# Two attention stages of a gated cross-attention block: rows on ScalarE's queue, ten pooled blocks, the maxima behind the value products

## The chip, the cores and the metric

The kernel runs on one core of one Trainium2 chip. The metric is the device time of one execution in microseconds; the time before is the median of three runs. The trace is of one further execution under the hardware profiler. TensorE does matmuls, VectorE, ScalarE and GpSimd the rest, and the sequencers of SyncE (SP) and GpSimd issue the DMAs.

## The reference

Two layers, each an attention and a mixture of experts, on x of 2 x 1024 x 512 in float32. Only the attention matters here. There are 16 heads of 32. Layer 0 adds a causal self-attention (1024 keys) and a cross-attention on a context of 2048 tokens; layer 1 has a cross-attention alone:

```python
att = einsum('bhqd,bhkd->bhqk', q, k) * scale
y   = einsum('bhqk,bhkd->bhqd', softmax(where(causal, att, -inf)), v)
y   = y + einsum('bhqk,bhkd->bhqd', softmax(einsum(qc, kc) * scale), vc)
```

## The kernel before, in words

The program runs in stages: projections, attention of layer 0 (`attn0`), its output and routing, experts, and the same for layer 1 (`attn1`). The change is in `attention` and in the class `Job`; both attention stages run it.

A unit is four heads of one batch entry. `attn0` has 16 units, causal and cross in turn; `attn1` has 8 cross units. A unit has four jobs of 256 queries, a job has steps of two key blocks of 128: a cross job has 8 steps, the causal jobs 1, 2, 3 and 4. That is 336 steps in `attn0` and 256 in `attn1`. The class `Plan` fixes, by an order written ahead of time, at which step each further piece of work is done.

In a step TensorE computes four score groups s0 to s3 (`scores`, L704): for one key block and two heads each, keys by queries, transposed, into one of three PSUM banks (`SC` = 3). The masks of the causal diagonal are added by small matmuls (L707). ScalarE takes the exponential of each bank into `probs` (L780), a ring of three steps (`RING`). A score group waits until the exponential three items back has left its bank; s2 of a step thus waits for the exponential of s3 of the step before. The step's value products (`values`, L721) follow one step late: four heads side by side in the array for each block, and after them, with a matrix of ones as weights (L728), the sums of the probabilities. Blocks listed in `job.pooled` have no ones products: GpSimd adds their probabilities up (L655, L658), and one ones group at the job's end (L736) takes the total in, after a wait for the last add. In the count of instructions each of these float32 matmuls is two, so that a group of four heads is eight.

The exponential needs the largest score of each query. TensorE computes scores a second time in another layout (`maxima`, L674, in PSUM `mx`, one buffer), and VectorE reduces them (L810). One group of maxima is 128 queries by up to 512 keys of four heads. The plan gives most steps one group, some two, the last none. They stand between s1 and s2. Two steps after a job's last group its maxima are turned by TensorE (`turn`, L687), written to SBUF by ScalarE (`turned`, L768), and set by DMA as an additional row, row 96, of the queries (`set_row`, L587), which stands against a row of ones in the keys. The first score group of a job waits for that row (L697). A drain of the job's sums (`drain`, L789), reciprocals (L827) and a product on GpSimd (L635) end a job.

SP issues, in its own order, the loads of the next units (`load_flat` for the maxima, `load_stack` in ten pieces for scores and values), the stores of results, and the rows. It holds no work of its own, but each issue stands behind the one before it and behind their waits.

Of the kernel before, what the change touches and what calls it, by code (L numbers as in the profile page):

```python
# [19 lines left out]
F32 = mybir.dt.float32  # L20
# [8 lines left out]
P = 128  # L29
B, T, D = 2, 1024, 512  # L30
TC, CC = 2048, 256
HEADS, HD = 16, 32
GH = P // HD
NG = HEADS // GH
UNITS = B * NG
BLK = 512
# [7 lines left out]
DMA = 16  # L44


class Phase:


    def __init__(self, nc, name):  # L50
        self.nc, self.name, self.stack, self.sems = nc, name, ExitStack(), []
# [329 lines left out]
QB = 256  # L381
STEP = 2
LEAD = 4
BUFS, TOPS, ROWS_DEEP = 2, 4, 10
# [9 lines left out]
class Job:  # L394
# [3 lines left out]
    def __init__(self, unit, u, qb, first):  # L398
        self.unit, self.u, self.qb, self.first = unit, u, qb, first
        if unit.causal:  # L400
            d = 2 * qb
            self.blocks = [(kb, 0, False) for kb in range(d)] + [(d, 0, True), (d + 1, P, True)]
        else:
            self.blocks = [(kb, 0, False) for kb in range(unit.keys // P)]
        self.steps = len(self.blocks) // STEP
        self.last = first + self.steps - 1
        self.groups = []
        for t in range(QB // P):
            n = (qb * (QB // P) + t + 1) * P if unit.causal else unit.keys
            self.parts = -(-n // BLK)  # L410
            for part in range(self.parts):
                cols = min(BLK, n - part * BLK)
                self.groups.append((t, part, cols, unit.causal and part == self.parts - 1))
        whole = [kb for kb, n0, masked in self.blocks if not masked]
        inner = [kb for kb in whole if kb < len(self.blocks) - 3]
        self.pooled = [kb for kb in inner if kb < 2 or kb % 2 == 0] if len(inner) > 2 else []

    def adds(self, step=None):

# [93 lines left out]
def attention(nc, name, c, units):  # L513
# [4 lines left out]
    plan = Plan(units)  # L518
    jobs, N_STEPS, N_JOBS = plan.jobs, plan.steps, len(plan.jobs)
# [3 lines left out]
    with Phase(nc, name) as ph:  # L523
        KS = [ph.sb(f"keys{b}", [P, GH, KEYS], F32R) for b in range(BUFS)]
        QS = [ph.sb(f"queries{b}", [P, GH, T], F32R) for b in range(BUFS)]
# [7 lines left out]
        topT = ph.sb("topT", [ROWS, TOPS, P], F32R)  # L533
# [12 lines left out]
        row_set = [ph.sem(f"row_set{d}") for d in range(ROWS_DEEP)]  # L546
        inverted = [ph.sem(f"inverted{d}") for d in range(DEEP)]
        y_out = [ph.sem(f"y_out{d}") for d in range(DEEP)]
        FLAT, STACK, ROW, PIECES = 2, 10, QB // P, 4

        def load_flat(sp, u, piece):
            unit, b = units[u], u % BUFS
            if piece == 0:
                sp.dma_start(KN[b][:, 0:unit.keys].bitcast(F32), unit.k_src[unit.row, :, 0, :]).then_inc(flat_in[b], DMA)
            else:
                sp.dma_start(QN[b][:, :].bitcast(F32), unit.q_src[unit.row, :, 0, :]).then_inc(flat_in[b], DMA)
# [20 lines left out]
        with nc.Block() as block:  # L577
            @block.sync
            def _(sp):
                def set_row(j):  # L580
                    job = jobs[j]
                    sp.wait_ge(exped, plan.turn_item[j] + 1)
                    if job.u >= BUFS:
                        sp.wait_ge(valued, plan.last_of[job.u - BUFS] + 1)
                    q0 = job.qb * QB
                    for t in range(QB // P):
                        sp.dma_start(QS[job.u % BUFS][3 * HD:3 * HD + 1, :, q0 + t * P:q0 + (t + 1) * P].bitcast(F32),  # L587
                                     topT[t * GH:(t + 1) * GH, j % TOPS, :].bitcast(F32)
                                     ).then_inc(row_set[j % ROWS_DEEP], DMA)

                def store(j):
                    d, job = j % DEEP, jobs[j]
                    sp.wait_ge(normed, j + 1)
                    sp.dma_start(job.unit.y_dst[job.unit.row, :, job.qb * QB:(job.qb + 1) * QB], y[d][:, :]
                                 ).then_inc(y_out[d], DMA)

                for piece in range(FLAT):
                    load_flat(sp, 0, piece)
                for piece in range(STACK):
                    load_stack(sp, 0, piece)  # L600
                for piece in range(FLAT):
                    load_flat(sp, 1, piece)
                for j in plan.turn_at[-1]:
                    set_row(j)
                for piece in range(STACK):
                    load_stack(sp, 1, piece)
                for m in range(N_STEPS + 8):
                    if 0 <= m - 7 < N_STEPS and plan.ends(m - 7) is not None:
                        store(plan.ends(m - 7))
                    for j in plan.turn_at.get(m, ()):  # L610
                        set_row(j)
                    for u in range(len(units) - BUFS):
                        piece = m - max(plan.unit_max_at[u], 0) - 1
                        if 0 <= piece < FLAT:
                            sp.wait_ge(max_ready, plan.unit_groups[u])
                            load_flat(sp, u + BUFS, piece)
                        for piece in range(2 * (m - plan.last_of[u] - 1), 2 * (m - plan.last_of[u])):
                            if 0 <= piece < STACK:
                                sp.wait_ge(valued, plan.last_of[u] + 1)
                                load_stack(sp, u + BUFS, piece)  # L620
                for d in range(DEEP):
                    sp.wait_ge(y_out[d], DMA * len(range(d, N_JOBS, DEEP)))
# [39 lines left out]
            def _(pe):  # L662
# [83 lines left out]
                    turn(j)  # L746
                for m in range(N_STEPS + 1):
                    if m < N_STEPS:
                        scores(m, 0)
                        scores(m, 1)  # L750
                        for k in plan.groups_at[m]:
                            maxima(k)
                        scores(m, 2)
                    if m:
                        values(m - 1)
                    if m < N_STEPS:
                        for j in plan.turn_at[m]:
                            turn(j)
                        scores(m, 3)

            @block.scalar
            def _(act):
                def turned(j):
                    item = plan.turn_item[j]
                    act.wait_ge(scored, item + 1)
                    if j >= TOPS:
                        act.wait_ge(row_set[(j - TOPS) % ROWS_DEEP], ROW * DMA * ((j - TOPS) // ROWS_DEEP + 1))
                    act.activation(topT[:, j % TOPS, :], sc[0:ROWS, item % SC, 0:P], ACT.Copy, scale=-1.0  # L768
                                   ).then_inc(exped, 1)

                def exponent(m, i):
                    job, item = jobs[plan.job_of[m]], plan.item[m, i]
                    _, n0, _ = job.blocks[(m - job.first) * STEP + i // 2]
                    if m >= RING and i == 0:
                        act.wait_ge(valued, m - RING + 1)
                        if plan.adds(m - RING + 1):
                            act.wait_ge(added, plan.adds(m - RING + 1))
                    act.wait_ge(scored, item + 1)
                    heads = slice(2 * (i % 2), 2 * (i % 2) + 2)
                    act.activation(probs[:, m % RING, i // 2, heads, n0:],  # L780
                                   sc[:, item % SC, :].rearrange("p (h q) -> p h q", q=QB)[:, :, n0:],
                                   ACT.Exp, scale=SCALE).then_inc(exped, 1)

                def drain(j):
                    d = j % DEEP
                    act.wait_ge(job_done, j + 1)
                    if j >= DEEP:
                        act.wait_ge(normed, j - DEEP + 1)
                    act.activation(both[d][:, :, :], acc[:, :, :], ACT.Copy).then_inc(drained, 1)  # L789

                for j in plan.turn_at[-1]:
                    turned(j)
                for m in range(N_STEPS + 1):
                    if m < N_STEPS:
                        for i in range(3):
                            exponent(m, i)
                    if m and plan.ends(m - 1) is not None:
                        drain(plan.ends(m - 1))
                    if m < N_STEPS:
                        for j in plan.turn_at[m]:  # L800
                            turned(j)
                        exponent(m, 3)

            @block.vector
            def _(dve):
# [745 lines left out]
```

## Time and profile before

| | |
|---|---|
| median of three runs | 4381.48 us (4379.73 to 4384.93) |
| profiled execution | 4377.09 us |
| its span | 4375.5 us |
| TensorE matmul busy | 3873.5 us, 89% |
| VectorE busy | 2522.5 us, 58% |
| ScalarE busy | 2009.5 us, 46% |
| GpSimd busy | 1417.7 us, 32% |
| ones products, L728 | 4928 instructions |
| adds on GpSimd, L655 and L658 | 80 and 408 |

A line of the page names the source line, the engine, the operation and output <- input; behind the count stand the busy time and the mean of one instruction in ns. Busy matmul time is modelled at its ends, so that a busy TensorE isn't one at its peak: short waits inside a step show as distances between starts, not as idle time.

### The profile page before, as it was taken

To read this page: it belongs to the slowest core of one execution; us is meant where nothing else is said; L and a number is where in the kernel's file an instruction comes from. 1 tells how busy PE (TensorE), PEld (TensorE's weight loads), DVE (VectorE), ACT (ScalarE), POOL (GpSimd) and SP (SyncE) were. 2 spreads that over 40 slices of the span, in tenths; PEclk is the share of its full clock that TensorE was granted. 3 is DMA by queue.
4 is the path that set the end of the run, shared out by engine and by line. 5 is a ranking of instruction groups with operands and counts; after the bars stand their busy time and mean duration, and the time that the engine had idled before them with its cause. 6 is when DMAs were issued, how large, how long until landed. Compare 5 with 4: busy or idle time off the path is not lost. (4 is left out here: it accounts for less than half of the span.)

```text
span 4375.5 us, 79396 instructions
## 1 busy us (share of the span) xinstructions
PE 3873.5 (89%) x32204; PEld 2714.2 (62%) x32204; DVE 2522.5 (58%) x2758; ACT 2009.5 (46%) x3511; POOL 1417.7 (32%) x718
## 2 busy tenths in 40 slices
PE   7989699999999997739996599999998739999997
PEld 5777456665665664429895355555555427888886
DVE  4345567767776773466664577777764464343342
ACT  2222256666666664016662266666655004444332
POOL 0000265555555554001110356666555000111110
PEclk9999699999999998759998799999999759999999
DMA  5478524423441431426663633322210413443331
GB/s 169 161 257 285 132 51 110 111 67 73 106 102 50 103 68 66 144 89 208 206 204 102 163 74 74 74 61 65 63 38 18 145 48 128 130 118 117 110 109 38
DMA packets 278320, 485.28 MB, mean 111 GB/s; under 512 B 21904, under 2 KB 117136, under 8 KB 269840
## 3 DMA queue, kind: packets, MB, share of 16 engines
q1 hardware_dynamic: 263952, 443.40, 35.3%
q0 software_dynamic: 14080, 37.76, 3.7%
q8 instruction: 215, 3.52, 0.4%
q14 instruction: 73, 0.60, 0.1%
HBM read 350.67 MB, written 130.02 MB: 110 GB/s over the span
## 5 line engine op out<-in xcount | busy, mean ns | idle before, releaser
L810 DVE TENSOR_REDUCE attn_parts<-attn_mx 128x4 f32<-128x2048 f32 (+2 forms) x608 | 1342.1, 2207 | 629.0 <-PE attn_mx L674 523.7
L780 ACT ACTIVATE attn_probs<-attn_sc 128x512 f32<-128x512 f32 (+1 forms) x2368 | 1227.7, 595 | 615.4 <-PE attn_sc L704 546.3
L658 POOL TENSOR_TENSOR attn_psums<-attn_psums,attn_probs 128x1024 f32<-128x1024 f32 x408 | 970.6, 2379 | 149.9 <-ACT attn_probs L780 115.6
L704 PE MATMUL attn_sc<-attn_queries,attn_keys 97*128 97x256 f32 (+1 forms) x4736 | 922.8, 313 | 50.2 <-DMA attn_queries<-attn_topT 42.8
L704 PEld LDWEIGHTS attn_sc<-attn_queries,attn_keys 97*128 97x128 f32 x4736 | 668.7, 193 | 402.9 <-issue 224.0
L721 PE MATMUL attn_acc<-attn_probs,attn_values 128*32 128x256 f32 x9472 | 644.9, 391 | 1.9 <-ACT attn_probs L780 1.4
L655 POOL TENSOR_TENSOR attn_psums<-attn_probs 128x1024 f32<-128x1024 f32 x80 | 190.6, 2382 | 790.2 <-ACT attn_probs L780 790.2
L1425 DVE TENSOR_TENSOR ffn_wL<-ffn_raw,ffn_wH 128x2048 fp32r<-128x2048 f32 x128 | 293.4, 2292 | 224.0 <-ACT ffn_wH L1380 222.7
L674 PE MATMUL attn_mx<-attn_keysn,attn_queriesn 32*128 32x512 f32 (+2 forms) x2432 | 312.5, 503 | 101.4 <-DVE attn_parts L810 72.8
L1380 ACT ACTIVATE ffn_wH<-ffn_raw 128x2048 fp32r<-128x2048 f32 x128 | 245.3, 1916 | 338.8 <-DMA ffn_raw<-in_L_ffn_W_dram 177.9
L721 PEld LDWEIGHTS attn_acc<-attn_probs,attn_values 128*32 128x32 f32 x9472 | 250.6, 110 | 188.9 <-issue 12.2
L728 PE MATMUL attn_acc<-attn_probs,keep_onesf 128*32 128x256 f32 (+1 forms) x4928 | 365.4, 385 | 0.0
L1337 PE MATMUL ffn_up<-ffn_xH,ffn_wH 128*128 128x256 f32 (+1 forms) x1024 | 348.4, 340 | 2.7 <-DVE ffn_xL L1431 2.7
L1337 PE MATMUL ffn_up<-ffn_xH,ffn_wL 128*128 128x256 f32 (+1 forms) x1024 | 348.8, 341 | 0.0
L1337 PE MATMUL ffn_up<-ffn_xL,ffn_wH 128*128 128x256 f32 (+1 forms) x1024 | 347.7, 340 | 0.0
L1352 PE MATMUL ffn_down<-ffn_wH,ffn_hH 128*128 128x512 f32 x768 | 306.7, 399 | 0.0
L1352 PE MATMUL ffn_down<-ffn_wH,ffn_hL 128*128 128x512 f32 x768 | 304.4, 396 | 0.0
L1352 PE MATMUL ffn_down<-ffn_wL,ffn_hH 128*128 128x512 f32 x768 | 304.3, 396 | 0.0
L1449 DVE TENSOR_TENSOR ffn_hL<-ffn_hf,ffn_hH 128x256 fp32r<-128x256 f32 (+1 forms) x256 | 138.2, 556 | 203.1 <-ACT ffn_hH L1401 202.4
L1306 POOL DMA_INDIRECT out_dram<-ffn_yo,ffn_idx_out x32 | 52.7, 1648 | 593.3 <-DVE ffn_yo L1460 463.3
L827 DVE RECIPROCAL attn_inv<-attn_both 128x64 f32<-128x64 f32 x384 | 200.8, 535 | 73.4 <-ACT attn_both L789 73.4
L674 PEld LDWEIGHTS attn_mx<-attn_keysn,attn_queriesn 32*128 32x128 f32 x2432 | 120.1, 188 | 195.1 <-DVE attn_parts L810 100.5
(190 smaller groups left out, 4424.9 us busy)
## 6 DMA issues: line engine op xcount, KB each, us to landing
ffn_raw<-in_L_ffn_W_dram SPq DMA_DIRECT2D x128, 1024.0 KB, 5.4
attn_keys<-l_cross_keys SPq DMA_DIRECT2D x48, 1024.0 KB, 12.7
attn_queries<-l_queries SPq DMA_DIRECT2D x48, 512.0 KB, 17.9
l_cross_keys<-projc_high SPq DMA_DIRECT2D x64, 256.0 KB
l_cross_keys<-projc_lowp SPq DMA_DIRECT2D x64, 256.0 KB
l_cross_values<-projc_vout SPq DMA_DIRECT2D x64, 256.0 KB
attn_keysn<-l_cross_keys SPq DMA_DIRECT2D x16, 1024.0 KB, 5.0
attn_values<-l_cross_values SPq DMA_DIRECT2D x64, 256.0 KB, 23.3
```

Of the source, the lines that this page charges most:

```text
L658: pool.tensor_tensor(ps, ps, at, ALU.add).then_inc(added, 1)
L674: mm = pe.matmul(mx[:, h, 0:cols], QN[b][rows_h, q0:q0 + P], KN[b][rows_h, part * BLK:part * BLK + cols], start=True, stop=True)
L704: mm = pe.matmul(out[:, n0:], KS[b][0:3 * HD + 1, h, kb * P:(kb + 1) * P], QS[b][0:3 * HD + 1, h, job.qb * QB + n0:(job.qb + 1) * QB], sta ...
L721: mm = pe.matmul(acc[h * HD:(h + 1) * HD, 0, n0:], VS[b][:, kb, h * HD:(h + 1) * HD], probs[:, m % RING, i, h, n0:], start=kb == 0, stop=k ...
L728: mm = pe.matmul(acc[h * HD:(h + 1) * HD, 1, n0:], c["onesf"][:, 0:HD], probs[:, m % RING, i, h, n0:], start=False, stop=False, skip_group ...
L780: act.activation(probs[:, m % RING, i // 2, heads, n0:], sc[:, item % SC, :].rearrange("p (h q) -> p h q", q=QB)[:, :, n0:], ACT.Exp, scal ...
L810: dve.tensor_reduce(parts[j % ROWS_DEEP][:, :, t, part], mx[:, :, 0:cols], AX.X, ALU.max).then_inc(max_read, 1)
L827: dve.reciprocal(inv[d][:, q0:q0 + QB // PIECES], both[d][:, 1, q0:q0 + QB // PIECES]).then_inc(inverted[d], 1)
L1337: mm = pe.matmul(up[ft % UP][:, 0:k], w[:, cols], x[:, ch, :], start=n == 0, stop=n == 3 * C - 1)
L1352: mm = pe.matmul(down[st][:, :], h[:, ft, st * P:(st + 1) * P], w[:, cols], start=ft == 0 and n == 0, stop=ft == FT - 1 and n == 2)
L1380: act.activation(wH[:, m % RING, :], raw[:, m % RING, :], ACT.Copy).then_inc(high_made, 1)
L1425: dve.tensor_tensor(wL[:, m % RING, :], raw[:, m % RING, :], wH[:, m % RING, :].bitcast(F32), ALU.subtract).then_inc(low_made, 1)
```

## The change

Four edits. `Job.pooled` gets longer: in a causal job all blocks without a mask, in a cross job blocks 0, 1, 2, 3, 4, 6, 7, 8, 10 and 12 (before: 0, 1, 2, 4, 6, 8, 10, 12). `set_row` leaves SP's program for ScalarE's, and stands behind the exponential of the fourth score group of the step in which the maxima were turned. The load pieces of a unit come three to a step, not two, where the unit between is a causal one. And TensorE's maxima of a step move from between s1 and s2 to behind the value products, ahead of `turn` and s3.

```diff
-        inner = [kb for kb in whole if kb < len(self.blocks) - 3]
-        self.pooled = [kb for kb in inner if kb < 2 or kb % 2 == 0] if len(inner) > 2 else []
+        self.pooled = whole if unit.causal else [kb for kb in whole[:-3] if kb < 4 or kb == 7 or kb % 2 == 0]
...
             def _(sp):
-                def set_row(j): ...
-                for j in plan.turn_at[-1]:
-                    set_row(j)
...
-                    for j in plan.turn_at.get(m, ()):
-                        set_row(j)
...
-                        for piece in range(2 * (m - plan.last_of[u] - 1), 2 * (m - plan.last_of[u])):
+                        pace = STACK // min(STACK, units[u + 1].keys // BLK + 1)
+                        for piece in range(pace * (m - plan.last_of[u] - 1), pace * (m - plan.last_of[u])):
...
                 for m in range(N_STEPS + 1):
                     if m < N_STEPS:
-                        scores(m, 0)
-                        scores(m, 1)
-                        for k in plan.groups_at[m]:
-                            maxima(k)
-                        scores(m, 2)
+                        for i in range(3):
+                            scores(m, i)
                     if m:
                         values(m - 1)
                     if m < N_STEPS:
+                        for k in plan.groups_at[m]:
+                            maxima(k)
                         for j in plan.turn_at[m]:
                             turn(j)
                         scores(m, 3)
...
             def _(act):
+                def set_row(j):
+                    job = jobs[j]
+                    act.wait_ge(exped, plan.turn_item[j] + 1)
+                    if job.u >= BUFS:
+                        act.wait_ge(valued, plan.last_of[job.u - BUFS] + 1)
+                    q0 = job.qb * QB
+                    for t in range(QB // P):
+                        act.dma_start(QS[job.u % BUFS][3 * HD:3 * HD + 1, :, q0 + t * P:q0 + (t + 1) * P].bitcast(F32),
+                                      topT[t * GH:(t + 1) * GH, j % TOPS, :].bitcast(F32)
+                                      ).then_inc(row_set[j % ROWS_DEEP], DMA)
...
                 for j in plan.turn_at[-1]:
                     turned(j)
+                for j in plan.turn_at[-1]:
+                    set_row(j)
...
                         exponent(m, 3)
+                        for j in plan.turn_at[m]:
+                            set_row(j)
```

## Rows read from the trace of the kernel before

**Rows 1.** Busy time by stage, first and second attention: stretch, length, engines, PEclk, DMA.

```profile
447.00:1707.00 1260.00, 1201.12 (x13266) 751.18 (x13265) 878.10 (x668) 745.05 (x1472) 676.67 (x328) 0.96 0.36 84
...
2440.00:3379.00 939.00, 870.30 (x9496) 518.15 (x9496) 645.18 (x410) 555.91 (x1089) 555.05 (x256) 0.95 0.28 65
```

**Rows 2.** Grouped lines by form, 2497 to 3349: busy us, mean ns | idle before.

```profile
L810 DVE TENSOR_REDUCE attn_parts<-attn_mx 128x4 f32<-128x2048 f32 x239 | 548.1, 2293 | 235.8 <-PE attn_mx L674 235.6
L780 ACT ACTIVATE attn_probs<-attn_sc 128x512 f32<-128x512 f32 x967 | 501.5, 602 | 242.3 <-PE attn_sc L704 242.3
L658 POOL TENSOR_TENSOR attn_psums<-attn_psums,attn_probs 128x1024 f32<-128x1024 f32 x182 | 433.3, 2381 | 51.1 <-ACT attn_probs L780 34.8
...
L635 POOL TENSOR_TENSOR attn_y<-attn_both,attn_inv 128x256 f32<-128x256 f32 x30 | 22.0, 734 | 0.0
```

**Rows 3.** Waits, second attention stage: us in total, times, longest.

```profile
PE attn_sc L704 <- DMA attn_queries<-attn_topT: 41.5, 7, 6.7
...
PEld attn_mx L674 <- DVE attn_parts L810: 34.6, 40, 2.9
```

**Rows 4.** Timeline of TensorE, a plain step: start us, us, instruction.

```profile
2595.31 0.97 PE L704 MATMUL attn_sc<-attn_queries,attn_keys 97*128 97x256 f32 x6
2596.22 0.51 PE L674 MATMUL attn_mx<-attn_keysn,attn_queriesn 32*128 32x512 f32 x4
2596.65 0.50 PE L704 MATMUL attn_sc<-attn_queries,attn_keys 97*128 97x256 f32 x2
2597.08 1.07 PE L721 MATMUL attn_acc<-attn_probs,attn_values 128*32 128x256 f32 x16
2597.97 0.61 PE L728 MATMUL attn_acc<-attn_probs,keep_onesf 128*32 128x256 f32 x8
2598.52 0.50 PE L704 MATMUL attn_sc<-attn_queries,attn_keys 97*128 97x256 f32 x2
```

**Rows 5.** Timeline of TensorE, a step without maxima, near the stage's end.

```profile
3359.82 0.98 PE L704 MATMUL attn_sc<-attn_queries,attn_keys 97*128 97x256 f32 x6
3361.01 0.50 PE L704 MATMUL attn_sc<-attn_queries,attn_keys 97*128 97x256 f32 x2 [0.21 <-ACT attn_probs L780]
3361.44 1.07 PE L721 MATMUL attn_acc<-attn_probs,attn_values 128*32 128x256 f32 x16
...
3362.88 0.51 PE L704 MATMUL attn_sc<-attn_queries,attn_keys 97*128 97x256 f32 x2
```

**Rows 6.** Timeline of TensorE at the second job of a unit.

```profile
2608.30 0.50 PE L704 MATMUL attn_sc<-attn_queries,attn_keys 97*128 97x256 f32 x2
2614.66 1.22 PE L704 MATMUL attn_sc<-attn_queries,attn_keys 97*128 97x256 f32 x4 [5.86 <-DMA attn_queries<-attn_topT]
...
2620.86 0.74 PE L704 MATMUL attn_sc<-attn_queries,attn_keys 97*128 97x256 f32 x4
```

**Rows 7.** Busy time behind that wait, and in steps without maxima; PEclk third from the end.

```profile
2614.00:2620.00 6.00, 5.34 (x38) 3.08 (x42) 2.29 (x1) 1.68 (x3) 0.00 (x0) 0.50 0.02 7
3359.00:3363.00 4.00, 3.79 (x53) 2.13 (x42) 0.00 (x0) 2.44 (x5) 3.71 (x3) 1.00 0.00 0
```

**Rows 8.** Timeline of TensorE, a step with masked scores.

```profile
676.62 0.62 PE L704 MATMUL attn_sc<-attn_queries,attn_keys 97*128 97x256 f32 x3
...
677.93 0.50 PE L674 MATMUL attn_mx<-attn_keysn,attn_queriesn 32*128 32x512 f32 x4
```

**Rows 9.** Timeline of SP's queue, 2575 to 2625: start of issue, its length.

```profile
2579.18 1.20 SPq L587 DMA_DIRECT2D attn_queries<-attn_topT  x2
...
2588.85 17.89 SPq L573 DMA_DIRECT2D attn_values<-l_cross_values  x4
...
2611.44 1.22 SPq L587 DMA_DIRECT2D attn_queries<-attn_topT  x2
```

**Rows 10.** Timeline of TensorE's weight loads in the plain step of rows 4.

```profile
2596.21 0.19 PEld L674 LDWEIGHTS attn_mx<-attn_keysn,attn_queriesn 32*128 32x128 f32 x4
...
2597.76 0.35 PEld L728 LDWEIGHTS attn_acc<-attn_probs,keep_onesf 128*32 128x32 f32 x8
```

More of the change, by code:

```diff
@@ L579, in _ @@
             def _(sp):
[L580 to L589, printed above, removed]
                 def store(j):
```

## The prediction

> **What bounds the kernel now.** The change touches only the two attention stages, so I first split the span by stage. They take 1260 and 939 us, 2199 of 4375.5 us, and TensorE is busy for 95% and 93% of them, at a granted clock of 0.96 and 0.95 [rows 1]. The grouped lines of the second stage show what stands beside it [rows 2]: ScalarE's exponentials are 602 ns each, four to a step, 2.4 us; one maximum on VectorE is 2.29 us, one to most steps; a GpSimd add is 2.38 us, seven to a job of eight steps. A step takes 3.21 us [rows 4]. So no engine but TensorE is full, and the order of its own work sets the step.
>
> How a step turns is in its timeline [rows 4]. Call a score group s0 to s3. From s3 of one step (2595.31) s0 and s1 follow at once, then the maxima (2596.22), s2 (2596.65), the value products (2597.08), the ones products (2597.97), and the next s3 at 2598.52: 3.21 us. The last steps of the second stage have no maxima left, and there s2 starts 1.19 us behind s3, after 0.21 us of idle time that ended with ScalarE [rows 5]: s2 may only start when the exponential of s3 is out of its bank. With maxima the same distance is 1.34 us [rows 4]. That is the key reading: the maxima are a block of 0.43 us (2596.22 to 2596.65), but they fill a wait that is there anyway, and cost the step 0.15 us.
>
> The waits of the second stage show the other loss: seven waits of TensorE, 41.5 us, for the row of maxima that SP's queue brings into the queries [rows 3]. In one of them [rows 6] s3 at 2608.30 is followed by nothing until 2614.66, and then the step from s0 to s3 takes 6.20 us, where at full clock it takes 3.73 (3.21 less the 0.34 from s3 to s0, and two more ones groups of 0.43), since the clock has fallen to half, 0.50 from 2614 to 2620 [rows 7].
>
> **Part 1, the maxima moved.** s0, s1 and s2 now stand together, so s2 is back at 1.19 us behind s3, as in the steps without maxima; the block of 0.43 us then stands between value products and s3, where nothing waits. Per step -0.15 + 0.43 = +0.28 us: 3.06 [rows 5] + 0.43 = 3.49 for 3.21. With no ones products the step comes to 3.06, still over the 2.9 us that one maximum and its block need on VectorE and TensorE in turn (2.29 + 0.5 + 0.1), so that loop doesn't bind. Steps with one maxima group: 242 in the second stage, 304 in the first, of which 30 have masked scores. There s0 and s1 run so long that the maxima begin at 677.93, 1.31 us behind s3 at 676.62 [rows 8]: nothing is hidden before, so nothing is lost. The 23 steps with two groups are set by VectorE either way; I give them +3 us in all. (242 + 274) x 0.28 = +144 us. Against it, the small waits of the maxima for VectorE, some 0.14 us in two steps of a job, vanish in the longer step: 34.6 us in 40 times of the weight queue in the second stage, most of it in the start-up steps [rows 3]; of it and its like in the first I take 10 + 8 = -18 us. Bounds of the price of a step: 0.06 (only 0.21 of the block, 512 columns at 2.4 GHz, is left) and 0.43 (nothing of the old place was hidden); I take 0.28, since both places are shown.
>
> **Part 2, more blocks pooled.** A cross job had 8 ones groups and has 6; a causal unit has 4 fewer, net of one final group for the second job. 64 x 2 + 8 x 4 = 160 groups of eight matmuls. One costs 0.43 us (the value products of two blocks run 2597.08 to 2597.97, and one ones group with the switch to s3, 0.1, to 2598.52) [rows 4]: -69 us. GpSimd gets 9 adds for 7 per cross job: 9 x (2.38 + 0.07) + 0.73 for normalizing [rows 2] = 22.8 us. The job will last 3 x 3.06 + 4 x 3.49 + 4.35 = 27.5 us, so GpSimd is at 83%. In its order (an add starts when its probabilities are there), the last add ends 22.9 us after the first probabilities and TensorE asks for the sum at 25. The ring of three probabilities keeps 1.5 us or more. In the fourth causal job it is not so: five adds in four short steps plus one normalize end at 13.0 us, TensorE is at the sum at 11.4: +1.6 us, eight times, +13. The second causal job loses a wait of TensorE for itself, -2.
>
> **Part 3, rows on ScalarE's queue.** SP's sequencer sat 17.89 us in the issue of four value loads, from 2588.85, and came to the row's two issues at 2611.44 [rows 9]. It does so after each of six unit starts. Read as above, the two steps behind lose 8.5 us in the first and up to 10.3, 57 together. On ScalarE's queue the row is issued behind the exponential of s3: at 0.6 and 1.2 us from that s3, if an issue takes the 0.6 us that it takes on SP (1.20 for two) [rows 9]. It is needed at the second s0, 0.34 + 3.49 = 3.8 us from s3. In the free case the row on SP was in time with issues at 2579.18 and need at 2582.3, 3.1 us; the new lead from first issue is 3.2. Beside the loads it may be late by half a us, six times: +3. So -57 + 3 = -54. The two issues hold ScalarE's next exponential back by 0.8 to 1.2 us; its three exponentials then end by 3.4 to 3.9 us, and the one of s3 can start at 4.0 in the new step. They are hidden, with 0.1 to 0.6 us to spare; in the old order they would not have been. Bounds: 0, and 1.2 x 96 = 115 us. SP itself loses 192 issues and has nothing late behind them. The new pace of the loads (three pieces for two in a causal unit) moves nothing on the path: SP's issues already run one behind the other.
>
> By the Trainium skill (Perfetto Trace Analysis, "DMA Instruction — HWDGE (DVE, Sync)") a sequencer that issues such a DMA locks a generator which two sequencers share. By that rule ScalarE would stand behind SP's long issues. No row here has two sequencers issuing.
>
> **The sum.** 144 + 3 - 18 - 69 + 13 - 2 - 54 = +17 us. The profiled execution took 4377.09 us (span 4375.5), 4.4 below the median of the runs; it would become 4394, and the median 4381.5 becomes 4398 us. Gains and price nearly cancel, and 0.05 us more or less per step is 26 us.
>
> **Rivals.**
> (B) Faster: the block is cheaper behind the value products. Ones products take up their weights under the products before them; if the maxima do so too, the block is 0.21 and not 0.43: -0.22 x 516 = -113, 4285 us; half of it 4341. It decides from 0.03 us per step on (17 / 516). For it: the weights of the ones products are taken up from 2597.76, 0.21 us ahead of their first matmul. Against it: those have the shape of the value products; the maxima's weights start at 2596.21, with the first matmul (2596.22), as those of every group of another shape do [rows 4, 10].
> (C) ScalarE's issue is held by SP's. In this trace's times the row of the second job would be issued 0.6 us behind the s3 before the one at 2608.30, at 2605.5, in the longer steps at 2606.5; SP is stuck until 2606.74 and free for the row at 2611.44 [rows 6, 9]. ScalarE then stands up to 5 us, six times: +30, 4428 us.
> (D) The row comes as late as before, since the same engines carry the loads: the 54 us are not won, 4452 us. Against it: what was late was the issue (2611.44), and TensorE went on 3.2 us after it, at 2614.66 [rows 6, 9].
> (E) GpSimd falls behind in every cross job, by 1 us at the sum: +64, 4462 us. For it: 83% busy and a ring of three. Against it: the margins above, and adds of even length, 2.38 us [rows 2].
> (F) The wait of 0.4 us that each step now has drops the clock. Against it: in the steps without maxima, which have such a wait, 1.00 was granted [rows 7].
>
> **Chances.** Forecast 0.52 (4375 to 4418), B 0.22, C 0.12, D 0.05, E 0.06, F 0.03. The range 4345 to 4435 takes in the forecast, C and a part of B. 0.2% is 9 us, about what a measurement of this kernel can tell. Below 4373: B and a little of the forecast, 0.25. Within: 0.2, from the forecast. Above 4390: the rest, 0.55.
>
> **What would show it.** Timeline of a plain step: s3 to s2 1.19, value products right behind s2, maxima block 0.43 ahead of s3, step 3.49 (one ones group) or 3.06. The ones products at 3584 instructions for 4928, 648 adds on GpSimd for 488. No wait for a row over 1 us in the second stage and its clock near 0.99. Waits of TensorE at the final sum of fourth causal jobs, 1.6 us. Wrong would be: plain steps under 3.4 (B), ScalarE's issues over 1 us each (C), waits at the final sum in cross jobs (E).

## The result, and the profile after

The changed kernel took 4473.2 us (median of four runs, 4470.0 to 4481.1), the kernel before 4382.8: ratio 1.0215, 95% interval 1.0203 to 1.0227. It is 90 us slower; forecast were 17 us (4398) and a range up to 4435. The direction was right, the size was not. The profiled execution took 4475.4 us, its span is 4473.6, 98.1 over the span before. In the spans the first attention stage, from first to last score group, grew from 1234 to 1302 us (+68), the second from 912 to 926 (+14), and the way up to each stage's first score by 8 us (+16), which makes 98.

Busy time of the changed kernel in the two stages, columns as in [rows 1]:

```profile
480.00:1782.00 1302.00, 1201.94 (x12445) 739.28 (x12445) 865.22 (x657) 744.44 (x1467) 892.73 (x422) 0.93 0.32 75
2547.00:3473.00 926.00, 845.71 (x8919) 497.40 (x8919) 631.25 (x403) 560.31 (x1085) 700.68 (x318) 0.96 0.26 58
```

The same query on the kernel before, from its first to its last score in the first stage:

```profile
472.30:1706.40 1234.10, 1189.82 (x13212) 744.13 (x13213) 865.11 (x657) 743.10 (x1468) 670.52 (x327) 0.97 0.35 82
```

Read the granted clock: 0.97 has become 0.93 in the first stage. Two levels are granted, 1.2 and 2.4 GHz, so half clock went from some 80 to 170 us there (83 and 173, added up from the clock records of the traces, as are all such sums below).

**A plain step** is as forecast. Timeline of TensorE after, the answer to [rows 4]:

```profile
2687.12 0.98 PE L689 MATMUL attn_sc<-attn_queries,attn_keys 97*128 97x256 f32 x6
2688.31 0.51 PE L689 MATMUL attn_sc<-attn_queries,attn_keys 97*128 97x256 f32 x2 [0.21 <-ACT attn_probs L775]
2688.74 1.07 PE L706 MATMUL attn_acc<-attn_probs,attn_values 128*32 128x256 f32 x16
2689.63 0.61 PE L713 MATMUL attn_acc<-attn_probs,keep_onesf 128*32 128x256 f32 x8
2690.18 0.51 PE L659 MATMUL attn_mx<-attn_keysn,attn_queriesn 32*128 32x512 f32 x4
2690.61 0.97 PE L689 MATMUL attn_sc<-attn_queries,attn_keys 97*128 97x256 f32 x6
```

s3 to s2 is 1.19 us, ended by ScalarE as in [rows 5]; the maxima take 2690.18 to 2690.61, 0.43; the step is 3.49 us for 3.21.

**The second job of a unit** still waits for its row of maxima. TensorE's timeline in the changed kernel, to be held beside [rows 6]:

```profile
2697.61 0.50 PE L689 MATMUL attn_sc<-attn_queries,attn_keys 97*128 97x256 f32 x2
2702.22 1.65 PE L689 MATMUL attn_sc<-attn_queries,attn_keys 97*128 97x256 f32 x6 [4.11 <-DMA attn_queries<-attn_topT]
...
2707.92 0.51 PE L659 MATMUL attn_mx<-attn_keysn,attn_queriesn 32*128 32x512 f32 x4
```

ScalarE there, with the issues of its queue:

```profile
2694.66 0.60 ACT L775 ACTIVATE attn_probs<-attn_sc 128x512 f32<-128x512 f32 x1
2694.72 1.20 ACTq L762 DMA_DIRECT2D attn_queries<-attn_topT  x2
2696.03 1.58 ACT L775 ACTIVATE attn_probs<-attn_sc 128x512 f32<-128x512 f32 x3 [0.78 <-PE attn_sc L689]
```

SP's queue there, to be held beside [rows 9]:

```profile
2676.73 18.02 SPq L572 DMA_DIRECT2D attn_values<-l_cross_values  x4
2694.80 5.33 SPq L582 DMA_DIRECT2D l_y<-attn_y  x1
```

ScalarE issued the row at once, two issues in 1.20 us, and its next exponential began 0.1 us behind them. The row was not there until 2702.2, 7.5 us after the first issue; in the kernel before it had been issued at 2611.44 and was in use at 2614.66, 3.2 us. All six such places of the second stage lose time as before: held against the same two steps of an undisturbed job, the two steps there are longer by 36 us in all, for 57 before.

**Behind a causal unit** the trace shows a second loss. TensorE in the first step of a cross unit:

```profile
1030.19 0.83 PE L713 MATMUL attn_acc<-attn_probs,keep_onesf 128*32 128x256 f32 x16
1032.81 0.64 PE L721 MATMUL attn_acc<-attn_psums,keep_onesf 128*32 128x256 f32 x8 [1.79 <-POOL attn_psums L643]
```

The busy time and clock of the 14 us behind it, and of another 14:

```profile
1034.00:1048.00 14.00, 13.79 (x88) 7.58 (x87) 8.20 (x6) 6.38 (x13) 12.45 (x6) 0.54 1.04 220
1050.00:1064.00 14.00, 13.27 (x143) 7.87 (x147) 10.73 (x8) 9.07 (x19) 10.14 (x5) 1.00 0.04 12
```

A wait of 1.79 us for GpSimd's last add, and then 14 us at 0.54, of which 13.7 at half clock: three steps of 4.8, 4.8 and 5.0 us (from value products to value products) where 3.06, 3.06 and 3.49 are due, 5 us lost. In the seven later cross units the wait stands seven times and the clock fell behind six of them, for 3.4 to 13.7 us; the first cross unit has both as well. The seven stretches together are 79 us at half clock.

**The stage's start:** ScalarE issues the six rows at once, SP has gone on to the second unit's loads, and the first score waits. SP's queue first:

```profile
459.17 24.49 SPq L572 DMA_DIRECT2D attn_values<-l_cross_values  x4
```

The last of these four issues, by itself:

```profile
468.77 14.89 SPq L572 DMA_DIRECT2D attn_values<-l_cross_values  x1
```

ScalarE's issues:

```profile
469.44 4.28 ACTq L762 DMA_DIRECT2D attn_queries<-attn_topT  x6
```

TensorE's first score:

```profile
479.98 0.55 PE L689 MATMUL attn_sc<-attn_queries,attn_keys 97*128 97x256 f32 x1 [10.58 <-DMA attn_queries<-attn_topT]
```

### The profile page after: what moved, and what is told of

It is laid out like the page before. It is cut to its first block and busy times, and to the rows that moved or that the text cites. A ratio compares the mean times of both kernels' runs of the same rounds, so it can differ in the third digit from the quotient of the medians.

```text
span 4473.6 us, 77148 instructions
## 1 busy us (share of the span) xinstructions
PE 3869.9 (87%) x30924; PEld 2693.4 (60%) x30924; DVE 2522.7 (56%) x2758; ACT 2019.3 (45%) x3511; POOL 1795.8 (40%) x878
## 5 line engine op out<-in xcount | busy, mean ns | idle before, releaser
L643 POOL TENSOR_TENSOR attn_psums<-attn_psums,attn_probs 128x1024 f32<-128x1024 f32 x560 | 1329.2, 2374 | 100.4 <-ACT attn_probs L775 33.5
L689 PEld LDWEIGHTS attn_sc<-attn_queries,attn_keys 97*128 97x128 f32 x4736 | 680.7, 196 | 382.7 <-ACT attn_probs L775 219.7
L706 PE MATMUL attn_acc<-attn_probs,attn_values 128*32 128x256 f32 x9472 | 664.8, 401 | 1.4 <-ACT attn_probs L775 1.4
L640 POOL TENSOR_TENSOR attn_psums<-attn_probs 128x1024 f32<-128x1024 f32 x88 | 209.0, 2375 | 579.4 <-ACT attn_probs L775 579.4
L713 PE MATMUL attn_acc<-attn_probs,keep_onesf 128*32 128x256 f32 (+1 forms) x3584 | 262.4, 386 | 0.0
```

Source lines behind the costliest of these rows:

```text
L640: pool.tensor_tensor(ps, probs[:, m % RING, 0, :, :], at, ALU.add).then_inc(added, 1)
L643: pool.tensor_tensor(ps, ps, at, ALU.add).then_inc(added, 1)
L689: mm = pe.matmul(out[:, n0:], KS[b][0:3 * HD + 1, h, kb * P:(kb + 1) * P], QS[b][0:3 * HD + 1, h, job.qb * QB + n0:(job.qb + 1) * QB], sta ...
L706: mm = pe.matmul(acc[h * HD:(h + 1) * HD, 0, n0:], VS[b][:, kb, h * HD:(h + 1) * HD], probs[:, m % RING, i, h, n0:], start=kb == 0, stop=k ...
L713: mm = pe.matmul(acc[h * HD:(h + 1) * HD, 1, n0:], c["onesf"][:, 0:HD], probs[:, m % RING, i, h, n0:], start=False, stop=False, skip_group ...
```

## The experiments

Each was timed in three rounds beside the kernel before; medians of before were 4378 to 4381 us in the four sessions. Unless told otherwise every kernel computes all of the reference.

| label | edit | us | ratio to before (95%) |
|---|---|---|---|
| e1_move_only | maxima moved | 4484.0 | 1.0233 (1.0214 to 1.0251) |
| e2_pool_only | pooled lists | 4396.9 | 1.0039 (1.0027 to 1.0051) |
| e3_rows_only | rows on ScalarE's queue | 4378.6 | 0.9996 (0.9986 to 1.0006) |
| e4_all_but_move | changed, maxima back | 4385.6 | 1.0011 (1.0000 to 1.0022) |
| e5_causal_five | changed, one add fewer | 4439.0 | 1.0133 (1.0116 to 1.0150) |
| e6_rows_start | e3, loads held at start | 4368.0 | 0.9978 (0.9968 to 0.9988) |
| e7_rows_spaced | e6, loads spaced | 4333.7 | 0.9898 (0.9881 to 0.9914) |
| e8_combined | e7, ten pooled (cross) | 4296.9 | 0.9814 (0.9798 to 0.9830) |
| e9_combined_move | e8, maxima moved | 4422.1 | 1.0096 (1.0077 to 1.0116) |
| e10_causal_all | e8, causal all pooled | 4330.9 | 0.9891 (0.9872 to 0.9910) |
| e11_causal_five | e8, causal five pooled | 4282.6 | 0.9779 (0.9761 to 0.9798) |
| e12_spaced_sp | before, loads spaced | 4322.4 | 0.9871 (0.9850 to 0.9891) |
| e13_move_pool_sp | changed, rows on SP, old load pace | 4466.6 | 1.0198 (1.0175 to 1.0221) |
| e14_five_sp | e11, rows on SP, no hold at start | 4287.4 | 0.9781 (0.9759 to 0.9803) |

**e1 to e4: one edit at a time.** The edits are those of the diff above: the block of `maxima(k)` alone (e1), the line of `self.pooled` alone (e2), `set_row` alone (e3), and all but the first (e4).

> The kernel before with one edit: the maxima behind the value products. Theory O (order): each of 516 plain steps costs 0.28 us more, as the trace after shows (3.49 for 3.21 with one ones group); less 18 us of small waits on VectorE: +126 us, 4508 us, of which at most 10 us through the clock. Rival W (what was missed in the forecast lies in this edit): the longer wait of each step also lowers the clock, or steps with masked maxima or two groups lose over 1 us each: +160 us and more. Rival N: most of the 91 us measured comes from the other two edits, and this one costs under 60 us.

> The kernel before with one edit: ten pooled blocks in a cross job, all unmasked blocks in a causal job. Gain from 160 fewer ones groups: -69 us. Theory P: in the shorter steps GpSimd is 90% busy in a cross job (22.8 of 25.2 us), the fourth causal job waits 2 to 3 us at its final sum, eight times, +20, and each such wait lowers TensorE's clock for 3 to 14 us, +2 to +7 each, +40: together about -10 us, 4372 us. Rival: the clock has nothing to do with it, -50 us, 4332 us.

> The kernel before with one edit: the rows on ScalarE's queue (the pace of the loads as before). Theory R: the row's packets stand on engines full of load packets, so the six waits of the second stage shrink from 57 to 36 us and not to 3; the two stage starts lose 8 us each since the loads of the second unit now go ahead of the first row: -21 + 16 = -5 us. The two issues on ScalarE, 1.2 us, aren't covered in the old order: 0.3 to 0.8 us for each of 96 jobs, +30 to +75. Sum +25 to +70 us. Rival: issues are hidden here too: -5 us. Rival of the forecast: rows free of the loads, -54 us.

> The changed kernel with the maxima back between s1 and s2. If the move costs 126 us here too: 4473 - 126 = 4347 us. If ScalarE's issues (hidden in the new order) come out in the old one and GpSimd binds in the shorter steps, the difference is smaller: 4380 to 4410 us. If the move is nearly free beside these (rival N), 4440 us and more.

Measured: +103, +16, -2 and +5 us against before. The move alone costs more than the whole change, and taking it out of the changed kernel gives 88. So the order is the main cost; rivals N and W are out. It costs less than 126 in e1 because it takes something from the row waits: the longer steps give the late row more time. Waits of TensorE for rows in the second stage (us in total, times, longest; before 41.5 in 7, [rows 3]), in e1:

```profile
PE attn_sc L704 <- DMA attn_queries<-attn_topT: 27.9, 7, 4.4
```

In e3:

```profile
PE attn_sc L689 <- DMA attn_queries<-attn_topT: 36.2, 7, 9.7
```

The six boundaries, where a unit's second job begins, lose 57 us before (two steps each, held against the same two of an undisturbed job), 35 in e1 and 44 in e3. e3 has the waits still and, at the stage starts, 7 and 5 us more: the sum is nothing. Its own expectation (+25 to +70, by issues on ScalarE that stand exposed in the old order) missed: an undisturbed cross job of the second stage lasts 26.4 us in both kernels, so the issues are hidden there too. The free row (-54) did not come about either. e2 was worse than both its lines (-10 and -50): in the old order VectorE's loop holds the steps without ones products. VectorE in e2 (timeline; the column in brackets is idle time before):

```profile
2651.53 2.29 DVE L809 TENSOR_REDUCE attn_parts<-attn_mx 128x4 f32<-128x2048 f32 x1 [0.16 <-PE attn_mx L673]
...
2654.44 2.29 DVE L809 TENSOR_REDUCE attn_parts<-attn_mx 128x4 f32<-128x2048 f32 x1 [0.15 <-PE attn_mx L673]
```

From one maximum to the next 2.91 us, where 2.78 were due (3.21 less the 0.43 of a ones group). Besides, its shorter steps made rows late on SP in ordinary jobs too (second stage; 17 waits for 7):

```profile
PE attn_sc L703 <- DMA attn_queries<-attn_topT: 48.1, 17, 7.1
```

And its waits for GpSimd's last add were there, with 180 us at half clock in the first stage for 83 before:

```profile
PE attn_acc L735 <- POOL attn_psums L657: 14.8, 9, 1.8
```

**e5 and e10: the wait for the last add, and the clock.**

```diff
-        self.pooled = whole if unit.causal else ...
+        self.pooled = whole[:5] if unit.causal else ...
```

> The changed kernel, but the fourth causal job pools five blocks, not six: one GpSimd add fewer there, so that TensorE's wait at its final sum (1.8 us, eight units) should go, for one ones group more (0.43 us each). Theory P (that wait starts the half-clock stretches of 3 to 14 us behind each causal unit, 90 us more at half clock in the first stage than before): -13 us of waits, +3 us, and -40 us of clock: about 4425 us, half clock in the first stage near 85 us again. Rival A (the clock falls because TensorE has fewer products to do in these steps, with or without the wait): 4463 us, half clock stays near 170 us.

> e8 with one edit: the causal jobs pool all unmasked blocks, as in the changed kernel. Four ones groups fewer per unit, -14 us; wait at the fourth job's final sum, 1.8 us, eight times, +14; and the clock behind it, 3 to 14 us at half, +30 to +45: 4330 us or more. If the clock loss belonged to the row waits or the short steps of the cross jobs: 4297 us.

e5 took one add and one wait of 1.8 us out of each causal unit: 34 us less than the changed kernel, of which the sum without clock explains 11 (1.8 - 0.43, eight times); 4425 us was expected. The first stage's clock:

```profile
480.10:1753.50 1273.40, 1187.04 (x12509) 734.26 (x12509) 865.27 (x657) 742.95 (x1467) 874.31 (x414) 0.95 0.33 76
```

0.95 for 0.93; the steps behind the causal units are at 3.06 and 3.49 in all seven later units. Rival A, too few products, asked for half clock near 170 us still. Half clock went to 135 us and not to the 85 expected; none of what is left stands behind a final sum of a causal unit. e10 does the reverse in a kernel without row waits: all unmasked blocks of the causal jobs pooled, four ones groups fewer per unit, are worth 14 us by the expectation's sum, and the kernel is 34 us slower, with the clock of the first stage down from 0.96 to 0.92. The first stage in e8:

```profile
475.20:1701.70 1226.50, 1178.72 (x12700) 731.46 (x12701) 865.14 (x657) 748.29 (x1468) 817.21 (x390) 0.96 0.34 82
```

And in e10:

```profile
473.00:1728.00 1255.00, 1196.45 (x12412) 738.04 (x12411) 864.21 (x657) 747.59 (x1463) 889.16 (x420) 0.92 0.33 80
```

**e6, e7 and e12: what makes the rows late.**

```diff
+                for j in plan.turn_at[-1]:
+                    sp.wait_ge(row_set[j], ROW * DMA)
                 for piece in range(STACK):
                     load_stack(sp, 1, piece)
...
+                        if units[u + 1].keys == TC:
+                            k = m - plan.last_of[u] - 2
+                            if k >= 0 and k % 3 == 0 and k // 3 < STACK:
+                                sp.wait_ge(valued, m)
+                                load_stack(sp, u + BUFS, k // 3)
+                            continue
```

The first hunk is e6, both are e7; e12 has the second alone, on the kernel before.

> The kernel before with the rows on ScalarE's queue, and SP holding back the second unit's loads at the start of each stage until the first rows have landed. Against the rows alone (4379 us): if the row waits of 10 us at the two stage starts come from these loads standing on the same engines, -12 to -14 us, 4366 us, and the first scores are again at 472 us. If the row is late for its issue on ScalarE, no change, 4379 us.

> As e6, and where the next unit is a cross one, the ten load pieces of a unit come one at a time, every third step, kept back until TensorE has reached the step, so that no row has a queue of load packets beside it. Theory R (the row's packets wait on the engines behind loads, whichever queue issues them): the six waits of the second stage go, with their half clock: 36 us less than e6, 4330 us. Rival (the row is late for its issue behind the exponential): waits of 1 us and more stay at these places, 4350 us and more.

> The kernel before with one edit: the loads spaced as in e7, the rows left on SP's queue. If the queue of load packets is the whole cause of the row waits, the rows need no other queue: as e7, 4333 us. If SP's place in the order also holds rows back (its stores and the waits of its loads stand ahead of them), waits of half a us and more remain: 4350 us.

e6 gave 11 us (for 12 to 14) and e7 another 34 (for 36): both as theory R has it. All pairs of steps at the six boundaries are at full length in e7 and e12. e12 is the surprise of the study: one edit of the load order, rows left on SP, is 58 us under the kernel before and 11 under e7, better than either line of its expectation. Its row waits in the second stage:

```profile
PE attn_sc L710 <- DMA attn_queries<-attn_topT: 3.5, 1, 3.5
```

Its SP queue where the second job of a unit begins:

```profile
2592.59 10.10 SPq L563 DMA_DIRECT2D attn_keys<-l_cross_keys  x2
2604.32 0.34 SPq L594 DMA_DIRECT2D l_y<-attn_y  x1
2609.26 1.22 SPq L587 DMA_DIRECT2D attn_queries<-attn_topT  x2
```

The 10.10 us are two pieces three steps apart, 0.3 us each, and not one long issue. The store and the row are issued at once (0.34 and 1.22 us; 4.61 for the store behind the packed loads), and the row lands in time. e7 stays 11 us behind e12: its second stage is 5 us longer, its first 2, and its waits for rows in the second stage are 7.1 us in 6, for 3.5 in 1. The rest is not explained.

**e8, e9 and e11: the price of the order by itself, and a faster kernel.**

> e7 with ten pooled blocks in cross jobs; the causal jobs pool as before, the maxima stand between s1 and s2. The old order gives 0.5 us per cross job of the 0.86 in ones products (VectorE's loop of 2.9 us holds the steps without ones products), 64 jobs: -32 us, 4300 us, if GpSimd keeps up (22.8 of 25.9 us). If its adds come late, -10 us only.

> e8 with one edit: the maxima behind the value products. Without row waits, final-sum waits and their clock, the price of the order stands alone. Theory O: cross job 27.4 for 25.9 us (3 x 3.06 + 4 x 3.49 + 4.35), 62 jobs with maxima, and 0.28 in six steps of eight causal units: +105 us, 4402 us. If part of the 103 us of e1 came from elsewhere (masked maxima, two-group steps): under +85 us.

> e8, but the causal jobs pool all unmasked blocks up to the fifth: three ones groups fewer per unit (-10 us), four adds in the fourth job, which end 0.5 us before TensorE asks: 4287 us if no wait appears, 4305 us or more if a short one still lowers the clock.

e8 came out as expected (-37 for -32). e9 measures the moved maxima without the long row waits: +125 us on e8, 20 over the expected 105. Half clock in the first stage grew there as well (110 to 149 us); at the rate seen above, 5 us lost in 13.7, that is an estimated 14 of the 20. Some of it begins behind waits of 2.40 us for VectorE, in steps with two groups of maxima, but e8 has these waits too, so what lengthens it stays open. e11 gives another 14 us with no wait at the sum, and is the fastest kernel of the study, 4282.6 us, 2.2% under the kernel before. It also separates the two causes that e5 and e10 change together: against e8 it has three ones groups fewer per causal unit, and half clock in the first stage went from 110 to 101 us; e10 takes away one more, which brings the wait back, and there it is 192 us.

**e13 and e14: ScalarE's queue inside the two ends.**

> The changed kernel with the rows back on SP's queue and the old pace of the loads. Forecast's step for the rows (-54 us in the changed kernel): 4527 us. Theory R (in the longer steps the row waits shrink to 35 us by themselves, as in e1, and ScalarE's queue adds 16 us at the stage starts): 4473 - 16 + 0 to 5 = 4457 to 4462 us. Between, if ScalarE's queue gives something here.

> e11 with the rows on SP's queue: e12 was 11 us below e7, so 4271 us if that carries over; if the shorter steps (0.5 us per cross job) make the rows late on SP, as the 17 small waits of e2 show, 4280 us or more.

In the changed kernel ScalarE's queue, with the new pace of the loads, costs 7 us (4473.2 against 4466.6, each against before 1.0215 and 1.0198, intervals that overlap): it is worth nothing there, and certainly not 54. The six boundaries lose 43 us in e13 and 36 in the changed kernel, so the queue won 7 there and gave back 16 at the stage starts. The new pace was not run by itself. In the shortest steps, with the loads out of the way, the queue makes no difference that shows: the ratios to before are 0.9779 (e11) and 0.9781 (e14), though e14 has 11 small waits for rows in the second stage, 6.0 us together, for one of 2.8. Its line of 4271 us did not come; the other, 4280 and more, did.

## Why the forecast was right and wrong

1. *The maxima moved, +144 + 3 - 18.* Right in mechanism and near in size: the plain steps are at 3.49 or 3.06, and in e9 the edit costs 125 us for 129. That the two are so close is in part luck, since some 14 of the 125 are an estimated loss of clock that no term held; the -18 for small waits on VectorE was not measured by itself. Rival B, whose break-even lay at 0.03 us per step, is refuted by the plain step: the block kept its 0.43. What I had not seen is that this cost and the row waits share time: with rows late, the edit costs 103 (e1), as 22 us of the waits go by themselves.
2. *More blocks pooled, -69 + 13 - 2.* Wrong, -17 measured (e13 against e1). The wait at the fourth causal job was forecast, 1.6 us, and measured 1.8. The step that failed is the price put on it: "+1.6 us, eight times, +13". It left out the clock behind the wait. Seven of the eight such waits were followed by half clock for 3 to 14 us, and e5, e10 and e11 show that the stretches come and go with the wait, not with the number of products. From e1 to e13 half clock in the first stage grew by 92 us (86 to 178); at 5 us lost in 13.7 this is an estimated 34 us. The shorter steps also let the row waits at the six boundaries grow again, 35 to 43 us. Forecast -58, with these 34 and 8: -16, for -17 measured. The stretch of [rows 6, 7] had shown just that behind a wait of 6 us; I carried it over to the long waits only.
3. *Rows on ScalarE's queue, -57 + 3.* Wrong, +7 measured (e13). The step that failed is the line under D: "what was late was the issue (2611.44), and TensorE went on 3.2 us after it". That issue stood last in the queue, when the load packets were nearly through, so its 3.2 us said nothing of a row issued in their midst; there it takes 7.5. The 57 us were too many besides: the longer steps of part 1 leave 35 of them (e1). The issue on ScalarE itself was as forecast, 1.20 us and hidden, and rival C did not appear. At the second job SP sat in four issues of 18.02 us together until 2694.75, and ScalarE's two went out at 2694.72 and after in the usual time. That row alone doesn't exclude the lock, since SP was at its end; but in the start-up ScalarE's six issues ran at 0.7 us each, 469.44 to 473.72, within a single issue of SP that lasted from 468.77 to 483.66. By the Trainium skill (Perfetto Trace Analysis, "DMA Instruction — HWDGE (DVE, Sync)") the generator is locked for exclusive use while an issue uses it. In these traces SP's long issue did not hold ScalarE's.
4. *The starts and the loads' order*, costed at nothing, took 16 us: SP had held the second unit's loads back behind the rows, as a side effect of its order. "SP itself loses 192 issues and has nothing late behind them" overlooked that the loads behind the rows would go out earlier, beside the first rows. These 16 us are part of what e13 measures for part 3.

Rivals E and F did not come about either: TensorE's only wait for GpSimd in the second stage is 0.9 us at its very end, and the plain steps from 1050 to 1064 have clock 1.00 with their short wait.

One edit upon the other (e1, e13, the changed kernel), the 90 us are 103 for the order, -17 for the pooling and +7 for the queue and the pace, 93 in sum since each was timed beside its own runs of the kernel before. The forecast had 129, -58 and -54. The shares depend on the way: alone, pooling costs 16 us (e2), and the order costs 88 beside the other edits (e4).

By the Trainium skill (DMA: Bandwidth & Descriptors, "Issuing engines are not separate DMA queues") DMAs of all issuing engines run on the same 16 DMA engines and interleave, and a second issuer saves only sequencer time. The traces agree: 7.5 us to the row's use from ScalarE's queue beside the loads, and all six waits at the boundaries still there, 36 us.

## What to carry to other kernels

Price a wait of TensorE with the clock behind it: here 1.8 us cost another 5 in several places, and the fix was one add less. Before a small urgent transfer is given another queue, see whether big ones are packed ahead of it on the engines; spacing those out (e12) won more than the queue. And a block of work that fills a wait is nearly free only where it stands: moved out, its full length comes due.

## What the runs showed of the hardware beyond that

SP's sequencer stayed in its issues while the DMA engines were full (17.89 us for four value loads, with a DMA share of 1.01 from 2588.85 to 2606.74, and then 4.61 us for a small store); with ten pieces spread over thirty steps the store took 0.34 (e12, at a share of 0.45 from 2600 to 2606). A wait of 1.8 us was followed by half clock in seven cases of eight in the changed kernel, while the 0.2 us in each plain step were not in the stretch from 1050 to 1064 (clock 1.00), whose steps have them.
